# Four units of the first feed-forward routed inside the memory stage instead of two, and the routing stages put in another order

## What is computed

```python
x = x + attn(_layernorm(x), ...)
x = x + ffn(_layernorm(x), ...)
x = x + mamba(_layernorm(x), ...)
x = x + ffn(_layernorm(x), ...)
```

```python
shared = silu(x @ sw1) * (x @ sw2) @ sw3
probs = softmax(x @ rw + rb)                 # 8 experts
w, idx = top_k(probs, 2)                     # two experts for each row
w = w / sum(w)
routed = sum over the two of w * ((silu(x @ ew1[e]) * (x @ ew2[e])) @ ew3[e])
return shared + routed
```

## Time and profile before

| | |
|---|---|
| time, median of three runs (lowest to highest) | 1785.74 us (1784.13 to 1794.47) |
| time of the profiled execution | 1792.23 us |
| its span | 1790.5 us |
| PE busy | 1362.6 us (76%) |
| DVE busy | 1266.3 us (71%) |
| ACT busy | 855.2 us (48%) |
| POOL busy | 880.4 us (49%) |

### The profile page before, as it was taken

How to read it: one execution, slowest core, us unless ns; L and a number is a source line. 1 busy time by engine, 2 the same in 40 slices (tenths; PEclk the granted TensorE clock), 3 DMA queues, 4 the chain that set the end, 5 groups by cost and what they waited for, 6 DMA issues and landing times. The chain is left out here.

```text
span 1790.5 us, 27815 instructions
## 1 busy us (share of the span) xinstructions
PE 1362.6 (76%) x8207; PEld 677.6 (38%) x8208; DVE 1266.3 (71%) x2981; ACT 855.2 (48%) x1215; POOL 880.4 (49%) x775
## 2 busy tenths in 40 slices
PE   3448999999999898785995777586676544584993
PEld 1213333333333265553994232131221200353992
DVE  3666899999989267674333279998998999573343
ACT  3403666666666734221553668467476332121551
POOL 3400212121211454675665248869869666475662
PEclk9655999999999999997997888698788656797996
DMA  4821111111112232254333395976957863624336
GB/s 121 265 73 48 53 49 55 47 58 44 61 47 65 54 84 84 86 159 108 85 93 111 98 226 154 249 182 162 245 131 199 198 163 94 174 87 124 111 93 166
DMA packets 218312, 210.68 MB, mean 118 GB/s; under 512 B 49247, under 2 KB 188482, under 8 KB 215874
## 3 DMA queue, kind: packets, MB, share of 16 engines
q1 hardware_dynamic: 196174, 180.70, 37.7%
q0 software_dynamic: 9216, 19.02, 3.3%
q10 hardware_dynamic: 12800, 9.46, 1.8%
HBM read 145.27 MB, written 63.37 MB: 117 GB/s over the span
## 5 line engine op out<-in xcount | busy, mean ns | idle before, releaser
L804 ACT ACTIVATE attn_prob<-attn_ps_cols 128x1024 f32<-128x1024 f32 (+1 forms) x320 | 292.0, 940 | 219.7 <-PE attn_ps_cols L680 218.7
L2546 POOL TENSOR_TENSOR ssm_hc<-ssm_h,ssm_cb 128x1024 f32<-128x1024 f32 x128 | 300.5, 2355 | 136.1 <-DVE ssm_h L2529 112.3
L2529 DVE TENSOR_TENSOR_SCAN ssm_h<-ssm_decay,ssm_ps_u 128x1024 f32<-128x1024 f32 x128 | 292.7, 2287 | 29.9 <-ACT ssm_decay L2517 12.6
L830 POOL TENSOR_SCALAR_AFFINE_SELECT attn_prob<-attn_prob 128x512 f32<-128x512 f32 x128 | 81.2, 635 | 415.7 <-ACT attn_prob L804 415.7
L712 DVE CUSTOM_DVE_ANT_0 attn_ps_rows<-attn_ps_rows,const_mask_rows 128x384 f32<-128x384 f32 (+3 forms) x512 | 236.1, 522 | 39.5 <-PE attn_ps_rows L647 37.3
L647 PE MATMUL attn_ps_rows<-attn_ks,attn_qs 72*128 72x512 bf16 (+3 forms) x768 | 228.8, 351 | 44.3 <-DMA attn_qs<-parts_dram 31.0
L2517 ACT ACTIVATE ssm_decay<-ssm_wide,ssm_aneg 128x1024 f32<-128x1024 f32 x128 | 146.1, 1146 | 173.5 <-DVE ssm_h L2529 97.1
L2480 PE MATMUL ssm_ps_u<-ssm_stack,ssm_spread 96*128 96x512 bf16 x256 | 99.1, 479 | 154.0 <-DVE ssm_h L2529 147.4
L680 PE MATMUL attn_ps_cols<-attn_qs,attn_ks 75*128 75x512 bf16 (+3 forms) x768 | 194.3, 333 | 4.6 <-DMA attn_qs<-attn_nrows 3.9
L699 PE MATMUL attn_ps_o<-attn_prob,attn_vw 128*32 128x512 f32 (+3 forms) x1536 | 166.6, 506 | 0.3 <-POOL attn_prob L830 0.3
L717 DVE TENSOR_REDUCE attn_nm<-attn_ps_rows 128x1 f32<-128x512 f32 x256 | 157.8, 682 | 7.8 <-PE attn_ps_rows L647 7.7
(11 more groups left out here) (361 smaller groups left out, 2438.6 us busy)
## 6 DMA issues: line engine op xcount, KB each, us to landing
ssm_wide<-delta_dram SPq DMA_DIRECT2D x128, 512.0 KB, 6.4
attn_ks<-parts_dram SPq DMA_DIRECT2D x48, 192.0 KB
attn_qs<-parts_dram SPq DMA_DIRECT2D x48, 192.0 KB
parts_dram<-proj_parts SPq DMA_DIRECT2D x8, 768.0 KB, 3.8
ffn1e_x<-ex_dram SPq DMA_DIRECT2D x40, 130.0 KB, 2.3
ffn2e_x<-ex_dram SPq DMA_DIRECT2D x40, 130.0 KB, 2.3
split_dram<-ssm_parts SPq DMA_DIRECT2D x6, 768.0 KB, 4.3
ssm_stack<-split_dram SPq DMA_DIRECT2D x18, 256.0 KB, 4.5
```

The lines of the kernel that those rows point to most:

```text
L804: nc.scalar.activation(prob[u % RING][:, heads[0]:heads[-1] + 1, 0:w], ps_cols[s % 2][:].rearrange("p b (x q) -> p (b x) q", x=len(heads) ...
L2529: nc.vector.tensor_tensor_scan(h[t % H_RING][:], decay[t % DECAY_RING][:], ps_u[t % 2][:], 0.0, ALU.mult, ALU.add).then_inc(scan_done, 1)
L2546: nc.gpsimd.tensor_tensor(hc[:, t % HC_RING, :], h[t % H_RING][:], cb[b % 2][:], ALU.mult).then_inc(hc_done, 1)
```

## The change

Three things change.

1. `AHEAD_UNITS` is 4 instead of 2: units 0 to 3 are routed in the memory stage, one every four blocks, by a table of first blocks (`STATS_AT` and others, unit u is 4u later). Scatters of units 0, 1 and 2 go out there at t = 16 to 27, two in every block; those of unit 3 come at the start of `route`. `rstd_pool` stands one block behind `mean_dve`. The store of a half stands one block earlier.
2. Turned rows get a tile for each unit (`xnT[u]`, eight instead of two), and the waits for reuse go.
3. `route` starts at unit 4 and has another order of work; a step takes the shared part of two units while there are units in store (`shared_in`). This order holds for the second feed-forward too, there with one unit to a step.

The core of the diff:

```diff
-TURNED_BEHIND = {5: 1, 7: 2}
+STATS_AT, NORM_AT, TURN_AT, LOGITS_AT, SETTLE_AT, TANH_AT, RANK_AT, SEND_AT = 9, 10, 11, 12, 13, 14, 15, 16
+def unit_at(t, first):
+    u, rest = divmod(t - first, HALF)
+    return u if rest == 0 and 0 <= u < AHEAD_UNITS else None
...
-                        for u in range(AHEAD_UNITS):
-                            sp.wait_ge(x1_stored[u], 16)
+                    if i >= 2:
+                        for u in (2 * i - 4, 2 * i - 3):
+                            sp.wait_ge(x1_stored[u % 2], u // 2 * 16 + 16)
                             sp.sem_inc(passed_sp, 1)
...
+                    u = unit_at(t, RANK_AT)
+                    if u is not None:
...
+                        pe.wait_ge(x1_ready, u + 3)
+                        rank_pe(nc, r, u)
                     outputs(t)
...
+                    u = unit_at(t, TURN_AT)
+                    if u is not None:
+                        pe.wait_ge(x1_ready, u + 2)
+                        pe.wait_ge(r.row_ready, u)
+                        pe.wait_ge(r.count_ready, u)
+                        turn_pe(nc, r, c, u)
...
-                    if t % HALF == 0 and half >= 2:
-                        store_x1(half - 2)
+                    if t % HALF == HALF - 1 and half >= 1:
+                        store_x1(half - 1)
...
-                    if t in (12, 15):
-                        rstd_pool(nc, r, pool, (t - 12) // 3)
-                    if 24 <= t < 28:
+                    if unit_at(t, NORM_AT) is not None:
+                        rstd_pool(nc, r, pool, unit_at(t, NORM_AT))
+                    if SEND_AT <= t < SEND_AT + (AHEAD_UNITS - 1) * HALF:
                         for j in range(2):
-                            scatter(nc, r, dram, pool, 0, (t - 24) * 2 + j)
+                            scatter(nc, r, dram, pool, (t - SEND_AT) // HALF, (t - SEND_AT) % HALF * 2 + j)
...
-AHEAD_UNITS, AHEAD_ENDS = 2, [1, 2, 3, 5, 7, UNITS_IN]
+AHEAD_UNITS, AHEAD_ENDS = 4, [1, 2, 3, 4, 5, 7, UNITS_IN]
...
+        def shared_in(s):
+            if not first:
+                return [s - 1] if s else []
+            done = 2 * (s - first)
+            return [u for u in (done, done + 1) if u < s] if s < UNITS_IN - 1 else [s - 1]
```

188 lines of the change are left out of this document (84 added, 104 removed).

## The result

| | before | after |
|---|---|---|
| median | 1791.6 us (20 runs) | 1798.8 us (20 runs) |
| ratio to before | 1 | 1.0039, 95% interval 1.0025 to 1.0053 |
| profiled execution, span | 1790.5 us | 1797.7 us |
| stage `memory` (first load to the next stage's first load) | 133.8 us | 153.2 us |
| stage `route` of the first feed-forward | 88.7 us | 75.3 us |

What follows compares the result with a forecast made beforehand. It took POOL's scatters to set the end of `route` and PE to bound the memory stage, POOL just below. `route` -16.0 and memory +11.6 gave -4.4 us: 1785.74 to 1781.3 us, range 1770 to 1793.

Steps and rivals of the forecast that it cites:

- Up to block 16: Memory stage up to POOL's mask of block 16: waits removed and a late load nearly cancel, +0.6 us.
- the two terms: Memory stage before block 16: 6.0 us saved on PE's waits for POOL, 7.2 us added by unit 0's late rows.
- Blocks 16 to 28: Memory stage, mask of block 16 to that of 28: POOL takes the lead, 56.2 us instead of 44.4, +11.8.
- The turns: POOL's own work in blocks 16 to 28 (masks, scatters, `rstd`, copy, sum): 51.1 us without any wait.
- unit 2's load wait: Memory stage, from block 18: unit 2's mean waits for rows loaded behind batch 3; POOL stands about 4 us.
- The fourth rival: Port contention: scatters beside the added norms in the memory stage take longer, +3 us, 1784 us; chance 0.05.
- PE alone would need some 47: Blocks 16 to 28 of the memory stage: PE by itself would need some 47 us, below POOL's 51.1.
- The far end: End of the memory stage's blocks 16 to 28: POOL is no longer 0.8 us ahead of PE, -0.8 us.
- `route`: Stage `route`: 16 scatters fewer on POOL, PE decides when units are placed, experts start earlier, -16.0 us.
- the last base's store: End of `route`: `name_experts` delays unit 7's base, whose store lands late; experts start at about 825.2, not 841.18.
- The rival that ended slower: Memory blocks 19 to 27: PE stays at its lower clock, 2.4 us more each, +17, 1803 us; lower clock's chance 0.12.
- no change above 1% was likely: Whole kernel: a chance of 0.85 to end between 1768 and 1804, within about 1% (18 us) of no change.

Runs made afterwards that it cites:

- before_rstd: The kernel before, with its two `rstd` of the memory stage one block later (blocks 13 and 16); ratio to before 0.9969.
- early_x: The kernel after, with SP loading the rows of units 0 and 2 ahead of batches 2 and 3; ratio to before 0.9989.
- sum_apart: The kernel after, with POOL's sums behind the mask of block 12 and the `rstd` of block 22 instead of masks 15 and 23; ratio to before 1.0041.
- scatters_last: The kernel after, with the 24 scatters of units 0 to 2 behind the mask of block 31; blocks 16 to 28 took 55.6 us, no ratio.
- send_later: The kernel after, with the scatters of units 0 to 2 starting one block later, at block 17; ratio to before 1.0029.
- late_wait: The kernel after, POOL waiting before unit 7's scatters in `route` until ACT's padding stores land; experts' first load 4.00 us behind the last scatter's start, no ratio.
- bias_earlier: The kernel after, with POOL's sum for a batch behind the mask of block 4 (12, 20) instead of 7 (15, 23); ratio to before 1.0049.

## Why the prediction was wrong, step by step

**Up to block 16: right.** Forecast +0.6, measured +1.1. The mean waited 6.26 (forecast 6.6), `products(12)` began 4.36 late at the lower clock, the two POOL waits were gone; before_rstd and early_x give the two terms apart: 5.6 and 8.0 us up to that mask, 6.0 and 7.2 in the forecast. (Their difference is 2.4 where 1.1 was measured; the 1.3 between are not assigned.)

**Blocks 16 to 28: the step that failed** is "that is 51.1 us without any wait ... Unit 0's labels are about 1 us late ... POOL then stands about 4 us": 5 us of waits. They were 11.2, and the stretch took 62.0 us instead of 56.2: 5.8 of the 7.7 us by which the memory stage was missed. The turns were right (50.8), unit 2's load wait smaller than said (1.91 instead of 4, as POOL came later by itself), and the waits for labels were 4.58 + 3.02 + 1.67 = 9.3 instead of 1. Behind this are two omissions. I never followed DVE's queue from the norm to the label (norm, three masks, place, `rows`, state, `make_e`, label), and I priced its instructions by rows of a kernel in which POOL stood idle beside them: 1.11 us for a norm that then took 1.11, 3.29, 2.54 and 4.85. The fourth rival named the lock, but in one direction only, with 1.1 us a norm: POOL's scatters held by DVE. In the runs POOL's mask and sum hold DVE, and for their whole length, while a scatter in the stretch took 0.96 to 1.06 us (the first one 1.23, as in before). How the 9.3 us of label waits divide between the queue and the hold was not measured. What the runs bound: with unit 1's norm free (sum_apart) the first label wait was 2.44 instead of 4.58, behind a mask that had waited 2.21 itself, and the second, 3.02, did not change.

**"PE alone would need some 47"** failed too as the length of the stretch: 55.6 in scatters_last, with PE busy 47.7. The 8 us are PE's waits: 3.39 and 3.41 ahead of turn(1) and turn(3), 0.75 ahead of turn(2). The forecast put no wait of PE on `place_dve` in this stretch. Freeing POOL of its label waits alone (send_later) fits that: by the ratios it brought 1.8 us, with intervals that overlap after's. With the norm of unit 1 free, PE's wait ahead of turn(1) is 1.2 us, so 2.2 of its 3.39 are the hold and the rest is DVE's order.

**The far end.** -0.8 was taken off for slack that wasn't there; the part behind the mask of block 28 grew by 0.6.

**`route`: right in size (-13.4 against -16.0), half right in cause.** The rank of unit 7 ended 58.1 us into the stage (forecast 55.5), the last scatter 3.5 late. The forecast then let the experts wait for the last base's store, 6.5 behind the last scatter; it was 5.58, and the reason is the landing of the scatters beside the stores (late_wait). That pads and base stores move under the last scatters when POOL's backlog shrinks was the thing that "is late next".

**Chances.** The rival that ended slower, PE falling to its lower level in each block, did not happen as told: the granted clock was 0.89 in the stretch, and the slow matmuls stand in two places, from 707.14 to 716.8 and from 736.58 to about 741. (Its 2.4 us a block use up 4.4 twice over from the fourth block on, not the fifth; nothing rests on it.) The measured +7 lies between my forecast and it, at a place for which no case had been worked out. The statement that no change above 1% was likely held.

## What to carry to other kernels

When work is moved beside a busy GpSimd, price VectorE's copies, casts, tensor-scalars and two-input instructions with the GpSimd instruction that may run beside them added in full, and look for the hold in an instruction's duration, since no wait shows it. Follow every queue from the moved work to what waits for it, not only the engine that seems to lead: here POOL's waits for labels, PE's for the count and the mean's for the rows each hid the gain of removing another, and four edits together (rows early, labels ahead, sums moved, scatters spread) took 16 of the stage's 153 us. A transfer that other work waits for is best issued ahead of the bulk loads as soon as its data is there.

## What the runs showed of the hardware that I had not expected

- One instruction of 128 x 128 values, 0.34 us by itself, took 4.08 us: it started beside the end of a scatter and stood through the mask and the sum that followed. So the hold passes from one POOL instruction to the next. An 8-column cast took 6.22 us beside a memset.
- TensorE's clock behind a wait is not told by the wait's length: behind 3.39 us (694.56) the matmuls ran at full speed, behind 0.63 us in after (707.14) and 1.07 in bias_earlier (645.87) `products` took 2.23 and 2.32 instead of 1.14. Nor is it the same for one wait at one place: ahead of turn(1) early_x waits 3.40 us like after, and its turn takes 1.09 instead of 0.63 and its `products` 2.09 instead of 1.14.
- A scatter's landing, from its start to the next stage's first load, was 3.8 to 4.0 us with the DMA engines free and 5.35 to 5.9, once 6.7 (sum_apart), with eight stores of 130 KB and two of 256 KB beside it or shortly ahead.
